# A decoder's future attention: normalised probabilities, a dense mixture of two heads per 32 rows, and an output over two blocks

## What is computed, cut to the first attention

```python
qkvf = h @ W_qkvf.T
q, k, v, f = split(qkvf, 4)                       # each (B, T, 256), then by heads
attn = einsum('bhtd,bhsd->bhts', q, k) * hs ** (-0.5)     # causal
up_future = einsum('bhtc,cdf->btfhd', f, W_conv)
k_future, v_future = up_future @ W_k.T, up_future @ W_v.T
future_attention = einsum('bhtd,bhtfd->bhtf', q, k_future)
sm = softmax([causal attn, future_attention])     # one softmax over both
new_x = sm_causal @ v + einsum('bhtf,bhtfd->bhtd', sm_future, v_future)
x = x + new_x @ W_proj.T
```

## Time and profile before

| what | value |
|---|---|
| runs without profile, us | 1718.21, 1712.42, 1714.85; median 1714.85 |
| profiled execution, its own time, us | 1716.57 |
| span of the profiled execution, us | 1714.6 |
| mean granted TensorE clock | 0.965 of full speed |
| busy share of the span: PE, PEld, DVE, ACT, POOL | 91%, 60%, 52%, 47%, 22% |
| instructions in the span | 34568 |

### The profile page before, as it was taken

One profiled execution on the slowest core, in us unless ns is written; L12 is line 12 of the kernel. 1 busy time (PEld: TensorE's weight loads), 2 busy tenths in 40 slices (PEclk: granted clock), 3 DMA queues, 4 the chain that ended last, 5 costly groups with the idle time before them and its releaser, 6 DMA issues. The chain is left out here.

```text
span 1714.6 us, 34568 instructions
## 1 busy us (share of the span) xinstructions
PE 1568.2 (91%) x13646; PEld 1024.7 (60%) x13646; DVE 892.1 (52%) x1863; ACT 812.9 (47%) x1585; POOL 371.5 (22%) x337
## 2 busy tenths in 40 slices
PE   8899999999799999999799999999787899899965
PEld 3455555555356666656565999999344666566642
DVE  4566666511555565555242211111273889667758
ACT  4355555533144544455431222222254788556666
POOL 0012222221100010000028300000721777311222
PEclk9999999999899999999789999999999899999988
DMA  7000000010200000000043799997379443000001
GB/s 264 1 1 2 1 1 2 22 34 1 85 20 11 20 20 20 20 11 2 14 162 126 227 328 329 326 326 238 94 193 219 118 95 88 12 12 12 2 1 44
DMA packets 148051, 150.16 MB, mean 88 GB/s; under 512 B 69890, under 2 KB 135106, under 8 KB 147890
## 3 DMA queue, kind: packets, MB, share of 16 engines
q1 hardware_dynamic: 144818, 140.60, 26.9%
q0 software_dynamic: 3072, 7.34, 1.4%
HBM read 120.40 MB, written 27.53 MB: 86 GB/s over the span
## 5 line engine op out<-in xcount | busy, mean ns | idle before, releaser
L2506 DVE TENSOR_TENSOR masked<-masked 128x512 f32<-128x512 f32 x70 | 49.8, 712 | 200.9 <-ACT masked L2408 200.9
L958 DVE CUSTOM_DVE_ANT_0 x_unused<-psum,masked 112x439 f32<-112x439 f32 x256 | 141.8, 610 | 20.3 <-PE psum L781 19.6
L896 ACT ACTIVATE x_probs<-psum,key_mask 125x448 f32<-125x448 f32 x192 | 106.1, 635 | 77.4 <-PE psum L801 77.4
L2349 PEld LDWEIGHTS psum<-mix_xb,mix_up 128*128 128x128 f32 x1120 | 130.6, 192 | 2.1 <-issue 0.4
L2349 PE MATMUL psum<-mix_xb,mix_up 128*128 128x128 f32 x1120 | 130.7, 275 | 0.0
L2359 PE MATMUL psum<-mix_down,masked 128*128 128x256 f32 x560 | 127.0, 380 | 0.1
L1477 PE MATMUL psum<-fold_full,hT 128*112 128x512 f32 x256 | 113.8, 597 | 1.3 <-DVE fold_part L1872 1.3
L2359 PEld LDWEIGHTS psum<-mix_down,masked 128*128 128x128 f32 x560 | 103.5, 190 | 13.4 <-DVE masked L2506 0.4
L1721 ACT COPY masked<-psum 112x448 f32<-112x448 f32 x128 | 63.8, 530 | 60.6 <-PE psum L1508 60.3
L781 PE MATMUL psum<-x_kT,x_qz 32*112 32x439 f32 x512 | 88.4, 591 | 3.2 <-DVE x_kT L943 3.2
L2408 ACT ACTIVATE masked<-psum 128x512 f32<-128x512 f32 x70 | 41.8, 597 | 97.1 <-PE psum L2349 97.1
(11 more groups left out here) (338 smaller groups left out, 3277.5 us busy)
## 6 DMA issues: line engine op xcount, KB each, us to landing
mix_up<-in_moe_up SPq DMA_DIRECT2D x35, 1024.0 KB
mix_down<-in_moe_down SPq DMA_DIRECT2D x35, 1024.0 KB
offset_rows<-join_rows SPq DMA_DIRECT2D x16, 784.0 KB, 5.7
hrow<-offset_rows SPq DMA_DIRECT2D x16, 784.0 KB, 5.2
x_ctx<-in_ctxT SPq DMA_DIRECT2D x16, 375.0 KB, 3.1
slots_x<-masked SPq DMA_DIRECT2D x1, 4480.0 KB, 21.4
mix_rows<-slots_x SPq DMA_DIRECT2D x35, 128.0 KB, 3.4
slots_y<-mix_result SPq DMA_DIRECT2D x35, 128.0 KB, 3.5
```

The lines of the kernel that those rows point to most:

```text
L896: nc.scalar.activation(probs[0:rows, 4 * (c % 2) + r], psum[0:rows, bank("tile", n, 4 * c + r), 0:G].rearrange("p (k t) -> p k t", k=4), A ...
L958: nc.vector.tensor_tensor_reduce(unused[:, at], psum[0:T, at, 0:KEYS], masked[0:T, n * KEYS:(n + 1) * KEYS], -1.0, -3.0 * NEG, ALU.add, AL ...
L2349: mm = nc.tensor.matmul(psum[:, 2 * u + half, m * BLOCK:(m + 1) * BLOCK], e_up[:, w, c, (half * H4 + m) * P:(half * H4 + m + 1) * P], xb[: ...
L2506: nc.vector.tensor_tensor(e_hidden[:, u, half * H4:(half + 1) * H4], e_relu[:, half], e_relu[:, half], ALU.mult).then_inc(hidden_ready.sem, 1)
```

## The change

- ScalarE still makes exponentials, but VectorE now sums them: `invert_sums(n)` sums the future probabilities, sums the 16 heads' 112 probabilities in one instruction of 112x1792 elements, adds both, takes the reciprocal and scales the future probabilities by it. It stands behind the centring and before `score_future(n + 1)`.
- GpSimd scales the probabilities in place, eight heads an instruction (`scale_probs`), two instructions a batch, before `weigh_future(n)`, which now waits for the scaled future probabilities. TensorE's turns wait for these multiplies.
- The shuffle, the logarithm, the exponential and GpSimd's old multiply go for this attention, and so do the ones beside the features.
- `v` is zero-filled with 2 x 128 columns for each half of the heads; even heads sit in the first 16 of 32 columns, odd heads in the last 16, so two heads add into the same 32 rows of the mixture. ScalarE copies the values in two instructions. The turns take even heads for even i, odd heads for odd i.
- The mixture has two blocks of 128 rows: two transposes of `fmix`, a copy of 224 columns, and an output over two blocks of contraction (`blocks = C`), which waits for the copy of the mixture. The output weight is not padded any more.

The core of the diff ("..." marks what is left out):

```diff
-            fmix = s.sb("fmix", [T, 2, H, 32])
+            fmix = s.sb("fmix", [T, 2, D])
+            fden = s.sb("fden", [T, 2, H])
+            summed, fadded, flipped, fscaled, scaled = s.counter("summed", 1), s.counter("fadded", 1), s.counter("flipped", 1), s.counter("fscaled", 1), s.counter("scaled", C)
...
-                pe.wait_ge(*exped.after(At(n), i))
+                pe.wait_ge(*(scaled.after(At(n), i // 2) if future else exped.after(At(n), i)))
                 if i >= 2:
                     pe.wait_ge(*copied.after(At(n), i - 2))
                 for k in range(HG):
-                    mm = nc.tensor.transpose(psum[0:T, 4 + i % 2, k * T:(k + 1) * T], probs[:, n % 2, HG * i + k], ident[0:T, 0:T])
+                    head = 8 * (i // 2) + 2 * k + i % 2 if future else HG * i + k
+                    mm = nc.tensor.transpose(psum[0:T, 4 + i % 2, k * T:(k + 1) * T], probs[:, n % 2, head], ident[0:T, 0:T])
...
-                        pe.wait_ge(*fsummed.after(At(n)))
-                        for g in range(NG):
-                            nc.tensor.matmul(psum[:, 7, g * T:(g + 1) * T], fmix[:, n % 2, HG * g:HG * (g + 1)].rearrange("p h e -> p (h e)"), ident[0:T, 0:T],
-                                             start=g == 0, stop=False, is_transpose=True, skip_group_check=True)
+                        for j in range(C):
+                            nc.tensor.matmul(psum[:, 7, j * T:(j + 1) * T], fmix[:, n % 2, j * P:(j + 1) * P], ident[0:T, 0:T],
+                                             start=j == 0, stop=False, is_transpose=True, skip_group_check=True)
...
+                    if future:
+                        j, at = i // 2, i % 2 * P + 32 * k
+                        mm = nc.tensor.matmul(psum[32 * k:32 * k + 32, 7, j * T:(j + 1) * T], v[0:T, n % NV, j, at:at + 32], turned[:, i, k, :],
+                                              start=False, stop=True, skip_group_check=True)
+                        continue
...
-                pe.wait_ge(*normed.after(At(n + 1)))
+                pe.wait_ge(*(mix_copied if future else normed).after(At(n + 1)))
                 for m in range(C):
-                    for g in range(NG):
-                        mm = nc.tensor.matmul(psum[:, 6, 2 * m * T:2 * (m + 1) * T], wt["wo"][:, g, m * P:(m + 1) * P], out_mixT[:, n % NM:n % NM + 2, g * T:(g + 1) * T], start=g == 0, stop=g == NG - 1)
+                    for g in range(blocks):
+                        mm = nc.tensor.matmul(psum[:, 6, 2 * m * T:2 * (m + 1) * T], wt["wo"][:, g, m * P:(m + 1) * P], out_mixT[:, n % NM:n % NM + 2, g * T:(g + 1) * T], start=g == 0, stop=g == blocks - 1)
                 mm.then_inc(projected.sem, 1)
...
-                nc.scalar.copy(v[0:T, n % NV, :, 0:HD], psum[0:T, 4, 0:D].rearrange("p (h d) -> p h d", h=H)).then_inc(v_read.sem, 1)
+                for e in range(2):
+                    dst = v[0:T, n % NV, :, e * P:(e + 1) * P].rearrange("p j (k x) -> p j k x", x=32)[:, :, :, e * HD:(e + 1) * HD]
+                    c = nc.scalar.copy(dst, psum[0:T, 4, 0:D].rearrange("p (j k e d) -> p e j k d", j=C, k=HG, e=2)[:, e])
+                c.then_inc(v_read.sem, 1)
...
-                nc.scalar.copy(mixT[:, n % NM], psum[:, 7, 0:G]).then_inc(mix_copied.sem, 1)
+                nc.scalar.copy(mixT[:, n % NM], psum[:, 7, 0:blocks * T]).then_inc(mix_copied.sem, 1)
...
-                if last and not offset and n <= NB:
+                if last and causal and n <= NB:
...
-                    take_logs(n - 1)
-                    invert(n - 1)
+                    if not future:
+                        take_logs(n - 1)
+                        invert(n - 1)
...
+            def invert_sums(n):
+                u = n % 2
+                dve.wait_ge(*fexped.after(At(n)))
+                dve.wait_ge(*fscaled.after(At(n - 2)))
+                nc.vector.tensor_reduce(fden[:, u], fprob[:, u].rearrange("p f h -> p h f"), X, ALU.add).then_inc(fsummed.sem, 1)
+                dve.wait_ge(*exped.after(At(n), NG - 1))
+                dve.wait_ge(*scaled.after(At(n - 2), C - 1))
+                nc.vector.tensor_reduce(rden[:, u], probs[:, u], X, ALU.add).then_inc(summed.sem, 1)
+                dve.wait_ge(*summed.after(At(n)))
+                dve.wait_ge(*fsummed.after(At(n)))
+                nc.vector.tensor_tensor(rden[:, u], rden[:, u], fden[:, u], ALU.add).then_inc(fadded.sem, 1)
+                dve.wait_ge(*fadded.after(At(n)))
+                nc.vector.reciprocal(rden[:, u], rden[:, u]).then_inc(flipped.sem, 1)
+                dve.wait_ge(*flipped.after(At(n)))
+                nc.vector.tensor_tensor(fprob[:, u], fprob[:, u], rden[:, u].unsqueeze(1).broadcast_to([T, FUT, H]), ALU.mult).then_inc(fscaled.sem, 1)
             def mix_future(n):
                 u = n % 2
-                if n == 0:
-                    dve.wait_ge(filled.sem, 2)
-                dve.wait_ge(*fexped.after(At(n)))
                 dve.wait_ge(*mixed.after(At(n - 2), 0))
-                nc.vector.tensor_reduce(fmix[:, u, :, HD:HD + 1].rearrange("p h e -> p (h e)"), fprob[:, u].rearrange("p f h -> p h f"), X, ALU.add).then_inc(fsummed.sem, 1)
                 dve.wait_ge(*fweighted.after(At(n)))
...
-                        if r == 1 and last:
-                            spread_denominators(n - 2)
                     combine(n)
                     for r in range(NG):
                         shift(n, r)
                     centre_future(n)
                     beside.dve_centre(dve, n, 6)
+                    invert_sums(n)
                     if n + 1 < NB:
                         score_future(n + 1)
                     mix_future(n)
...
+            def scale_probs(n, j):
+                pool.wait_ge(*flipped.after(At(n)))
+                pool.wait_ge(*exped.after(At(n), NG - 1))
+                some = slice(8 * j, 8 * j + 8)
+                x = probs[:, n % 2, some]
+                nc.gpsimd.tensor_tensor(x, x, rden[:, n % 2, some].unsqueeze(2).broadcast_to([T, 8, T]), ALU.mult).then_inc(scaled.sem, 1)
...
-                pool.wait_ge(*fexped.after(At(n)))
+                pool.wait_ge(*fscaled.after(At(n)))
...
-                if n >= 2:
+                if n >= 2 and not future:
                     normalise(n - 2)
+                if n < NB and future:
+                    for j in range(C):
+                        scale_probs(n, j)
...
-        a0 = Weights(nc, "a0", areas[0], {"wk": fm("a0_wk", D), "wq": fm("a0_wq", D), "wvq": fm("a0_wvq", 2 * D), "wo": wide("a0_wo")})
+        a0 = Weights(nc, "a0", areas[0], {"wk": fm("a0_wk", D), "wq": fm("a0_wq", D), "wvq": fm("a0_wvq", 2 * D), "wo": fm("a0_wo", D)})
...
-    f["a0_wo"] = padded_rows(t(i["L0_attn_W_proj"]))
+    f["a0_wo"] = t(i["L0_attn_W_proj"])
```

More of the change, by code:

```diff
@@ L1366, in token_attention @@
         NM = 2 if offset else 4
-        mixT = qz_all[:, 0, 0].rearrange("p (u t) -> p u t", t=G) if causal else s.sb("mixT", [P, NM, G])
+        mixT = qz_all[:, 0, 0].rearrange("p (u t) -> p u t", t=G) if causal else s.sb("mixT", [P, NM, C * T] if future else [P, NM, G])
         if offset:
@@ L1370, in token_attention @@
         kT = cross.kT if causal else s.sb("kT", [P, 2, 2, G])
-        v = room[0][:, 0:NV * H * 32].rearrange("p (u h d) -> p u h d", u=NV, h=H) if causal else s.sb("v", [P, NV, H, 32])
+        v = room[0][:, 0:NV * H * 32].rearrange("p (u h d) -> p u h d", u=NV, h=H) if causal else s.sb("v", [P, NV, C, 2 * P] if future else [P, NV, H, 32])
         rowmax = s.sb("rowmax", [T, 2, H])
@@ L1411, in token_attention @@
         out_mixT = gmixT if offset else mixT
+        blocks = C if future else NG
         def factor_load(sp, n):
@@ L1553, in output_of_last @@
                 bank = 4 + n % 2
-                pe.wait_ge(*normed.after(At(n)))
+                pe.wait_ge(*(mix_copied if future else normed).after(At(n)))
                 for m in range(C):
-                    for g in range(NG):
-                        mm = nc.tensor.matmul(psum[:, bank, m * T:(m + 1) * T], wt["wo"][:, g, m * P:(m + 1) * P], out_mixT[:, n % NM, g * T:(g + 1) * T], start=g == 0, stop=g == NG - 1)
+                    for g in range(blocks):
+                        mm = nc.tensor.matmul(psum[:, bank, m * T:(m + 1) * T], wt["wo"][:, g, m * P:(m + 1) * P], out_mixT[:, n % NM, g * T:(g + 1) * T], start=g == 0, stop=g == blocks - 1)
                 mm.then_inc(projected.sem, 1)
@@ L1663, in _ @@
         def _(act):
-            for x in (exped, copied, mix_copied, logged, inverted) + ((k_read,) if not causal else ()) + ((v_read, qm_read, vf_read, fexped) if future else (cross.k_read,) if offset else ()):
+            for x in (exped, copied, mix_copied) + ((logged, inverted) if not future else ()) + ((k_read,) if not causal else ()) + ((v_read, qm_read, vf_read, fexped) if future else (cross.k_read,) if offset else ()):
                 x.start(act)
@@ L1996, in _ @@
                         take_cross_queries(1, 0)
```

(15 more changed lines are left out.)

9 lines of the change are left out of this document (4 added, 5 removed).

## The result

| | before | after |
|---|---|---|
| median of 20 runs | 1716.60 us | 1724.51 us |
| lowest, highest | 1711.71, 1726.62 | 1715.83, 1730.94 |
| span of the profiled execution | 1714.6 | 1720.6 |
| mean granted clock | 0.965 | 0.959 |

The ratio is 1.0036, 95% interval 1.0024 to 1.0048: some 6 us slower. That is just over the prediction's bound of 0.3%, and the interval lies on both sides of this bound.

What follows compares the result with a forecast made beforehand. TensorE bounded the future attention before; a new ring of 15.5 us plus extras would bound nearly every batch after, ending the stage at 343.05 against 338.27, +4.8 us: 1720 on the median, range 1716 to 1724, 8 in 10 1705 to 1735.

Steps and rivals of the forecast that it cites:

- The ring: Future attention: each batch goes round VectorE, ScalarE, VectorE, GpSimd, VectorE in 15.5 us; with extras 250.1 us over 15 rounds.
- The extras: VectorE work behind mix_future: queries 7.2 us, additions 3.6, norm scalings 4.0; also centrings 0.6 and delayed exponentials 2.2.
- What TensorE could do: TensorE's own rounds in the future attention after the change: 15.1 and 16.5 us, mean 15.8.
- The rival of the hidden ring: At mix_future against the next batch's maxima, ring under 14.8 us stays hidden behind TensorE; about 1696 us; chance 0.2.
- The tail: Stage end: mix_future of batch 15 15.8 us after its maximum, addition 0.65, then 8.3 to the last output; end 343.05.
- passing them on one to one: Next stage starts on TensorE behind the future attention's last output, so its 4.8 us delay reaches the total in full.
- The lock between two engines: VectorE's future scaling against GpSimd's first multiply: whoever is first delays the other, GpSimd by 0.2 us or VectorE by 1.7.
- The rate in the Trainium skill: GpSimd's 896-element multiply at about 2.6 cycles per element: 1.94 us, ring 16.0, some 6 us worse; the rows were preferred.
- Clock: Rival: TensorE's idle spells lower its clock, ten in rounds and one in the tail; +8 us, 1728; chance 0.07.

Runs made afterwards that it cites:

- e8: Kernel after with GpSimd's weighing done twice in every batch, all others waiting for the second; ratio to before 1.0217, rounds 281.8 us.
- e1: Kernel after with GpSimd weighing the future values before it scales the probabilities; 1709.45 us, ratio to before 0.9942.
- e3: Kernel after with each GpSimd scaling taking 4 heads and not 8, half of the probabilities left unnormalised; 1711.37 us, ratio to before 0.9959.
- e2: Kernel after with VectorE taking the queries before mix_future; 1719.31 us, ratio to before 1.0006.
- e7: Kernel after with 12 unused matmuls in TensorE's wait before the last norm sums; 1724.20 us, ratio to before 1.0014.
- e10: Kernel after with the next batch's future scores ahead of the sums on VectorE; 1823.32 us, ratio to before 1.0606.
- e5: Kernel after with GpSimd's weighing before its scalings and VectorE's queries before mix_future; 1711.12 us, ratio to before 0.9938.
- e6: Kernel after with GpSimd's weighing first and only 4 of each 8 heads scaled; 1708.87 us, ratio to before 0.9920.
- e9: Kernel after with GpSimd's weighing first and 8 unused matmuls in TensorE's wait before the last turns; 1707.72 us, ratio to before 0.9935.
- e11: Kernel after with next batch's future scores ahead of the sums on VectorE and GpSimd's weighing before its scalings; 1795.25 us, ratio to before 1.0446.

## Why the prediction was right, step by step

The prediction gave 1720 us, 4.8 us later. Against the two medians it is 7.9, against the spans 6.0, by the ratio 6.2.

- **The ring** held in mechanism and size, within the scatter of a trace's rounds. Groups of the kernel after, 88 to 312 us (count, busy us, mean ns, idle before):

```profile
L2059 POOL TENSOR_TENSOR fold_part<-fold_part,a_rden 112x896 f32<-112x896 f32 x28 | 47.1, 1700 | 154.1 <-DVE a_rden L1924 154.1
...
L1919 DVE TENSOR_REDUCE a_rden<-fold_part 112x16 f32<-112x1792 f32 x14 | 28.1, 2010 | 0.2 <-issue 0.2
L1932 DVE TENSOR_REDUCE a_fmix<-masked 112x256 f32<-112x1024 f32 x13 | 25.2, 1942 | 29.4 <-POOL masked L2094 29.4
L2094 POOL TENSOR_TENSOR masked<-masked,a_fprob 112x1024 f32<-112x1024 f32 x13 | 25.1, 1928 | 0.0
...
L1924 DVE RECIPROCAL a_rden<-a_rden 112x16 f32<-112x16 f32 x14 | 3.5, 252 | 0.5
```

  Multiply 1.70 for a forecast 1.7, wide sum 2.01 for 2.05, a plain round 15.4 to 15.5 for 15.5, first to last maximum 250.8 for 250.1. The wait ahead of `mix_future` is 2.43 us for some 2. e8 moves the rounds up by what it adds, and e1 and e3 move them down to TensorE's own pace.
- **The extras** held where e2 tests them, 7.2 us of queries. One effect was overlooked: TensorE's second turn waits for the queries, which now stand behind `mix_future`. It shows as 4.6 us in three waits (PE L1512 on L1831 above). A fourth stands at 83 us. With them the clock falls, which the forecast did not have in the rounds either. The cost was small: the round of batch 1 takes 17.0 us, 0.3 above what the sum gives it, and that of batch 5 18.0, 0.7 above. It isn't the same in each execution. In e7 such a wait stands at 236 us, the clock is 0.60 and 0.55 from there to 244 us, and the round of batch 10 takes 17.0 us for 15.4 in the kernel after. So a part of the 7.2 us of e2 is clock and not queries; which part was not separated.
- **What TensorE could do** without the ring was 15.8 us a round in the prediction; e1 shows 234.5/15 = 15.6. The rival of the hidden ring had the gain right in kind and wrong in size: 1696 was forecast, and e1, which brings its condition about by another order (13.2 us of ring by its expectation, where the rival needed under 14.8), gives 0.9942, some 10 us below before and not 20. 13.9 of it lie in the rounds, and 3.6 are lost in the tail.
- **The tail** is the term that was mis-sized, with 8.3 us for what took 12.6. `mix_future` of the last batch ends 15.7 us after the maximum (forecast 15.8) and the addition at 333.64. Then 8.3 us were forecast for the rest from the rows of before, where the clock was full. e7 with the clock at 0.92 and above takes 8.33, so the missing 4.3 us of this execution are the clock: it falls inside TensorE's 5.0 us of idleness and is 0.50 until 343 us, with L1575 in 5.19 us and not 3.27. The size is that of one execution. The same stretch took 9.9 us in e2 and 10.4 in e10, both behind the same wait of 5.02 us, 10.4 in e8 behind 7.03 us, and 12.6 in e5 where e1 took 10.2 behind the same waits. So the clock cost 1.6 to 4.3 us in the eleven traces without a fill in that place, and the length of the wait does not order them; what does stays open. The prediction had this only in a rival, "plus one in the tail". Its own sum let TensorE wait there for the addition and then took the 8.3 us at full clock: this is the step that failed.
- **Errors that cancel.** The first maximum lies 1.6 us earlier than in the trace of before, which the forecast did not have; over all traces it lies between 66.6 and 71.2 us, in no order that follows the edits, so part of this is the execution and not the change. That the stage end came within 3.3 us of the forecast is partly luck. Rounds +0.7, tail +4.3, start -1.6, small terms -0.1: 3.3 us, which is the difference between a stage end of 346.3 and the forecast 343.05. The stages behind gave back 2 of the 8 us; passing them on one to one was too much.
- **The lock between two engines** was too dear. GpSimd's first multiply overlaps VectorE's scaling of the future part, which takes 0.23 us alongside. In the view of the tile over batches 2 and 3 (ns, min/median/max) the kernel after has

```profile
L2059 POOL TENSOR_TENSOR fold_part<-fold_part,a_rden x3: 1678/1722/1722, 108.4 to 124.2; 112x896 f32<-112x896 f32 x3
```

  where the 1722 are first multiplies and 1678 is a second one. In the same batches of e1, where none overlaps it, they are 1683 to 1686. The overlap costs 0.04 us, not 0.2, and nothing of 1.7 us shows in the kernel after. What the Trainium skill, SBUF — State Buffer, "SBUF: two separate sides", says of an exclusive lock is therefore not to be seen at this place: the scaling was not held back. Elsewhere something like it is. In the runs with the weighing first (e1, e5, e6, e9) GpSimd's second multiply of batch 12 runs beside VectorE's scaling of the norm (L285 and L289), and both are stretched. In e1 the multiply takes 3.50 us, where the median of all 32 is 1.68, and one L289 1.76, where the median is 0.51; TensorE's turn then waits 0.77 us for the multiply (timeline of e1):

```profile
270.75 3.50 POOL L2059 TENSOR_TENSOR fold_part<-fold_part,a_rden 112x896 f32<-112x896 f32 x1
...
272.74 1.76 DVE L289 TENSOR_SCALAR hT<-hT,ln 128x448 f32<-128x448 f32 x1
```

  So a delay of the size that the prediction feared does occur, but between other operations, and no run tests what held them. The rate in the Trainium skill, GPSIMD Engine Reference, section 3.1, would have made the multiply an estimated 1.94 us; it took 1.70.
- **Clock** as the cause of the whole: no. The rounds ran at 0.93 to 1.00 (windows of some 32 us; in windows of 4 us it dips to 0.53), the rows of VectorE and GpSimd have the same durations in all of them (the wide sum 2.01 throughout), and e1 takes 16.3 us from them by an order on GpSimd alone.

Open: where the first 1.6 us and the returned 2 us come from, what lengthens e5's rounds beyond the 1.5 us, how long the clock stays low behind a wait, and the share of clock in e8 and e11.

## What to carry to other kernels

When a step is moved into a loop of three engines, write the loop out once and look at the order on the engine in its middle: what the next one waits for goes first, what only TensorE needs later goes behind. Here this order alone, with nothing computed less, turned 0.4% slower into 0.6% faster. A move that fills a wait pays only while that wait is there (e2 against e5), and at the end of a stage a wait of a few microseconds can cost TensorE a second time, in clock, here 1.6 to 4.3 us, from one execution to the next.

## What the runs showed of the hardware that was not expected

The clock fell to 0.50, 1.2 of 2.4 GHz, within TensorE's idle 5.0 us in the kernel after, and was back at 1.00 only 9.8 us after work had begun again (333.69 to 343.5 us). In e2, behind the same wait and over the same work, it was back 3.3 us after (326.71 to 330.0). In e7 it fell while TensorE was busy with unused matmuls, some 1.5 us behind a wait of 2.36 us. In the rounds of the kernel after, waits of 1.64 to 2.65 us for the queries were enough to stand before a fall to 0.50. The Trainium skill, TensorE: Matmul & The Clock Gate, "Part 1: The HAM clock gate", describes a clock that is halved when the engine goes idle; the traces agree in that a wait of TensorE stands before each of these falls.

GpSimd's multiply of 112x896 with a broadcast operand overlapped a VectorE operation on SBUF operands for 0.2 us at a cost of 0.04 us. In e1 the same multiply took 3.50 us beside VectorE's scaling of the norm, and 1.68 elsewhere.
